# Top-k attention: the steering rounds moved from ScalarE's tile counts to TensorE differences with one Sign per head

## Chip, cores and metric

One core of a Trainium2 chip runs the whole program. The metric is the device time of one execution in microseconds (us), lower is better. The kernel before takes 3272.49 us (median of 3 runs, 3266.62 to 3277.44).

## What is computed

A block over 32 batches of 256 tokens and 256 features: a layernorm, a cross attention with 16 heads of 16 features in which each query keeps only its 64 highest scores, a gated residual, a second layernorm, an 8-bit float matrix product with bias, and a second gated residual.

```python
scores = jnp.einsum('bhqd,bhkd->bhqk', Q, K) / sqrt(d)          # 256 x 256 per batch and head
topk_scores, topk_idx = jax.lax.top_k(scores, 64)
probs = jax.nn.softmax(topk_scores, axis=-1)
attn = einsum('bhqk,bhqkd->bhqd', probs, gather(V, topk_idx))
x = x + tanh(g_xattn) * (attn @ Wo.T + bo)
x = x + tanh(g_ffn) * ffn_fp8(layernorm(x))
```

## The kernel before, in words

**Groups and tiles.** Half of a batch's heads (8 of 16) make a *group*; there are 64 groups, numbered `i`. A head has 256 queries by 256 keys of scores, which are two *tiles* of 128 queries by 256 keys, so a group has 16 tiles (`GT`). `score_sb` holds four groups of tiles (`RING`) in the SBUF, queries on the partitions.

**Finding the 64th score.** For every query row a threshold `X` is looked for in four steering rounds (`GUIDES`), `r` = 0 to 3. A round counts how many scores of each row lie above `X` and moves `X` toward the count 60.5 (`AIM`) by a Newton or a chord step. After the four rounds the scores above `X` are counted once more and the eight next lower ones are picked with MAX8 (`following`); count and place give the 64th score exactly, `thr`. Rows whose 64th and 65th scores tie are *unsure* and are settled by a slow path (`settle`, `select_tile`).

**Who does what.** In `guide_counts` (L880) ScalarE counts 15 of the 16 tiles of a round: a `Sign` of X minus the tile, with `accum_out` as the count. VectorE counts the 16th (L1068). VectorE then moves the thresholds in `update_thresholds` (L1083 to L1121), a chain of up to eight dependent steps on 16 or 32 columns, between whose steps two `copy_scores` are placed. `final_tiles` (VectorE) makes for four tiles a round a compare with count (L1146), one pass over 1024 columns that turns the scores above X into -3e38 (L1151), and four MAX8 (L1157). `final_thresholds` closes a group.

ScalarE also makes the masks, `unfit` = Relu(thr - score), (`masks_of`, L891) and the exponentials `pT_sb` (`exps`, L900), and evacuates the projections, the mixed values and the MLP. TensorE computes the scores (`scores`, L698), the transposed scores with the masks added times `dropb` (`exponents`, L712 and L716), the product with the values (`mix`, L731, in float32, recorded as two matmuls each), and the projections. VectorE copies the scores from the PSUM with their row maximum (`copy_scores`, L1047). SP moves the operands through DRAM; GpSimd does layernorms and splits operands into bf16 parts.

**Order.** All orders are written out by hand, one stream for each engine, with semaphores between them. While VectorE finishes group `i`, the rounds steer group `i + 1`, the scores of group `i + 2` are copied, and group `i - 1` is masked, exponentiated and mixed. So a batch is eight rounds long (`g` = 0, 1; `r` = 0 to 3), and the program has 256 of them. Each round of ScalarE is:

```python
                        if guided:
                            guide_counts(2 * b + g + 1, (2 * p + g + 1) % RING, r)
                        for n in (2 * r, 2 * r + 1):
                            if mixes:
                                masks_of(2 * mb + mg, 2 * mp + mg, n)
                                mixing(mb, mp, mu, mg, n, has(-1))
```

and TensorE does in it, for two heads, scores, exponents and mix, plus one of the projections in some rounds. In the PSUM, `ps_s` (scores) and `ps_e` (exponents) have two banks each, and `ps_o`, `ps_a`, `ps_b`, `ps_x` one each.

## Time and profile before

| | before |
|---|---|
| median of 3 runs | 3272.49 us |
| the profiled execution's own time | 3268.81 us |
| its span | 3266.9 us |
| busy: VectorE, ScalarE | 2691.6 us (82%), 2730.3 us (84%) |
| busy: TensorE matmuls, weight loads | 1780.4 us (54%), 950.5 us (29%) |
| busy: GpSimd | 966.1 us (30%) |
| mean granted TensorE clock | 0.717 of 2.4 GHz |

Busy time is the union of an engine's instructions; it does not say which engine the others wait for. Instructions of one engine overlap by a part of their latency, so a group's mean duration is longer than the step from one start to the next, and a sum over a stream has to be made with steps between starts. TensorE's clock is granted at one of two levels, 0.50 (1.2 GHz) or 1.00 (2.4 GHz); a number between them for a stretch is a mean over time.

### The profile page before, as it was taken

The numbers are of one execution on the slowest core, as the hardware profiler recorded it, in microseconds if no ns is written. First come the engines' busy times: TensorE is split into PE (matmuls) and PEld (weight loads), VectorE is DVE, ScalarE is ACT, GpSimd is POOL, SyncE is SP. The second block draws the span as 40 slices with busy tenths as digits, with TensorE's granted clock in tenths as the row PEclk, the third lists the DMA queues.
The fourth block names the chain that finished last, engine by engine and source line by source line (L and its number), as shares of the span: only waits on it lengthen the run. The fifth ranks groups of instructions, "written<-read, shape, count | busy, mean of one in ns | idle before, by whom it ended". The sixth has DMA issues, their size and how long they took to land.

```text
span 3266.9 us, 51511 instructions
## 1 busy us (share of the span) xinstructions
PE 1780.4 (54%) x7952; PEld 950.5 (29%) x7952; DVE 2691.6 (82%) x11883; ACT 2730.3 (84%) x9638; POOL 966.1 (30%) x1174
## 2 busy tenths in 40 slices
PE   3245555555465555455556556564556556454555
PEld 2122233332233233232323333332233223232222
DVE  1678888888888888888888888888888888888884
ACT  1888888998788898797889998988798788997983
POOL 5122223233222233232233223333223233232112
PEclk8567677777677777776667777767676767777777
DMA  4223332223333223331233333223333133331211
GB/s 70 38 43 60 49 47 52 52 49 63 52 52 54 45 49 63 52 55 34 48 64 56 60 48 56 48 48 64 53 49 55 33 62 61 55 54 33 40 24 46
DMA packets 451902, 166.43 MB, mean 51 GB/s; under 512 B 245616, under 2 KB 451440, under 8 KB 451520
## 3 DMA queue, kind: packets, MB, share of 16 engines
q1 hardware_dynamic: 451136, 162.38, 28.4%
q14 instruction: 310, 2.54, 0.3%
q8 instruction: 72, 1.18, 0.2%
q0 software_dynamic: 384, 0.33, 0.1%
HBM read 102.57 MB, written 59.24 MB: 50 GB/s over the span
## 4 chain that ended last, share of the span: by engine, by line
DVE 36%; ACT 30%; issue 17%; PE 14%; DVEq 2%; POOL 1%; ACTq 0%; DMA 0%; SPq 0%; POOLq 0%; another core or an unknown queue 0%
ACT act_junk L880 22%; DVE masked L1151 5%; DVE score_sb L1047 4%; PE ps_o L731 4%; DVE following L1157 4%; DVE masked L1146 3%; ACT unfit L891 3%; ACT pT_sb L900 2%; PE ps_a L684 2%; DVE X L1083 2%; PE ps_b L675 2%; PE ps_e L712 1%; PE ps_a L686 1%; DVE chord L1115 1%; PE ps_e L716 1%
## 5 line engine op out<-in xcount | busy, mean ns | idle before, releaser
L880 ACT ACTIVATE act_junk<-score_sb,X 128x256 int8<-128x256 f32 x3840 | 1892.1, 503 | 211.3 <-DVE X L1121 183.2
L712 PE MATMUL ps_e<-qs,ks 99*128 99x256 bf16 x1024 | 348.2, 350 | 1321.7 <-ACT pT_sb L900 1321.7
L731 PE MATMUL ps_o<-pT_sb,v_aug 128*32 128x256 f32 x2048 | 766.4, 514 | 0.5 <-ACT pT_sb L900 0.5
L880 ACT ACTIVATION_READ_ACCUMULATOR act_junk<-score_sb,X 128x1 f32 x3840 | 755.0, 197 | 0.0
L891 ACT ACTIVATE unfit<-score_sb,thr 128x256 bf16<-128x256 f32 x1024 | 463.1, 504 | 218.0 <-DVEq L1241 214.6
L1047 DVE TENSOR_SCALAR_CACHE_REDUCE score_sb<-ps_s 128x256 f32<-128x256 f32 x1024 | 418.8, 415 | 142.1 <-PE ps_s L698 140.0
L712 PEld LDWEIGHTS ps_e<-qs,ks 99*128 99x128 bf16 x1024 | 121.9, 119 | 1403.6 <-ACT unfit L891 1199.5
L1146 DVE TENSOR_SCALAR_CACHE_REDUCE masked<-score_sb,X 128x256 f32<-128x256 f32 x1024 | 426.3, 472 | 19.1 <-DVE x_res L1294 8.4
L1157 DVE MAX8 following<-masked 128x8 f32<-128x256 f32 x1024 | 357.7, 409 | 1.7 <-issue 0.7
L540 POOL CAST split<-proj 128x512 bf16<-128x512 f32 x64 | 48.0, 750 | 1042.8 <-ACT proj L866 1027.2
L716 PE MATMUL ps_e<-dropb,unfit 128*128 128x128 bf16 x2048 | 355.9, 273 | 0.0
L1151 DVE SCALAR_TENSOR_TENSOR masked<-masked,score_sb 128x1024 f32<-128x1024 f32 x256 | 336.8, 1316 | 0.4
L900 ACT ACTIVATE pT_sb<-ps_e 128x512 f32<-128x512 f32 x512 | 301.7, 590 | 11.9 <-PE ps_o L731 11.8
L731 PEld LDWEIGHTS ps_o<-pT_sb,v_aug 128*32 128x32 f32 x2048 | 231.9, 136 | 266.4 <-issue 191.0
L716 PEld LDWEIGHTS ps_e<-dropb,unfit 128*128 128x128 bf16 x2048 | 253.3, 124 | 52.4
L698 PE MATMUL ps_s<-ks,qs 96*128 96x256 bf16 x1024 | 228.2, 311 | 67.7 <-DVE score_sb L1047 35.1
L1083 DVE TENSOR_TENSOR X<-aim,count 128x16 f32<-128x16 f32 x256 | 82.3, 322 | 200.8 <-ACT act_junk L880 167.3
L510 POOL TENSOR_SCALAR var<-mv 128x2 f32<-128x2 f32 x64 | 14.6, 228 | 579.4 <-DVE mv L994 576.5
L1068 DVE SCALAR_TENSOR_TENSOR dve_junk<-score_sb,X,minus_twos 128x256 bf16<-128x256 f32 x256 | 158.2, 618 | 0.1
L698 PEld LDWEIGHTS ps_s<-ks,qs 96*128 96x128 bf16 x1024 | 74.8, 102 | 269.8 <-issue 206.2
L602 POOL TENSOR_TENSOR rest<-y_sb,magic_sb 128x512 f32<-128x512 f32 x32 | 43.9, 1371 | 362.4 <-DVE magic_sb L1020 362.4
L559 POOL COPY qs<-rows 96x4096 bf16<-96x4096 bf16 x32 | 127.2, 3974 | 22.7 <-DMA rows<-q_scr 11.6
(158 smaller groups left out, 3332.8 us busy)
## 6 DMA issues: line engine op xcount, KB each, us to landing
rows<-q_scr SPq DMA_DIRECT2D x192, 128.0 KB, 5.1
rows<-k_scr SPq DMA_DIRECT2D x192, 128.0 KB, 5.0
o_scr<-o_sb SPq DMA_DIRECT2D x128, 128.0 KB, 2.7
q_scr<-split SPq DMA_DIRECT2D x32, 384.0 KB, 2.7
k_scr<-split SPq DMA_DIRECT2D x32, 384.0 KB, 2.7
x_in<-in_x SPq DMA_DIRECT2D x32, 256.0 KB, 3.1
ctx_sb<-in_ctx SPq DMA_DIRECT2D x32, 256.0 KB, 2.7
v_scr<-proj SPq DMA_DIRECT2D x32, 256.0 KB, 5.8
```

What stands on the lines that cost most here:

```text
L698: ins = nc.tensor.matmul(ps_s[:, n % 2, jh * TOK:(jh + 1) * TOK], qs[u][0:SPLITS, h, 8 * jh:8 * jh + 8, :].rearrange("d j t -> d (j t)"), ...
L712: nc.tensor.matmul(ps_e[:, n % 2, kc * TOK:(kc + 1) * TOK], ks[u][:, h, 8 * kc:8 * kc + 8, :].rearrange("d j t -> d (j t)"), qs[u][:, h, : ...
L716: ins = nc.tensor.matmul(ps_e[:, n % 2, kc * TOK + jh * P:kc * TOK + jh * P + P], unfit[:, n % MASKS, jh, kc * P:kc * P + P], dropb[:], st ...
L731: ins = nc.tensor.matmul(ps_o[32 * c:32 * c + 32, half * TOK:(half + 1) * TOK], v_aug[p][:, 2 * h + kc, :], pT_sb[:, n % 2, kc * TOK:(kc + ...
L880: ins = nc.scalar.activation(act_junk[:, t, :], score_sb[:, slot, t, :], ACT.Sign, scale=-1.0, bias=X[slot % 2][:, 0, t:t + 1], accum_out= ...
L891: ins = nc.scalar.activation(unfit[:, n % MASKS, jh, :], score_sb[:, slot, t, :], ACT.Relu, scale=-1.0, bias=thr[:, slot, t:t + 1])
L900: nc.scalar.activation(pT_sb[:, n % 2, :], ps_e[:, n % 2, :], ACT.Exp).then_inc(s_PT, 1)
L1047: ins = nc.vector.tensor_scalar(score_sb[:, slot, t, :], ps_s[:, n % 2, jh * TOK:(jh + 1) * TOK], 0.0, None, ALU.add, ALU.max, accum_out=m ...
L1068: ins = nc.vector.scalar_tensor_tensor(dve_junk[:, t - ACT_TILES, :], score_sb[:, slot, t, :], X[slot % 2][:, 0, t:t + 1], minus_twos[:].t ...
L1146: nc.vector.tensor_scalar(masked[:, k, :], score_sb[:, slot, t, :], X[slot % 2][:, 0, t:t + 1], None, ALU.is_gt, ALU.add, accum_out=final_ ...
L1151: nc.vector.scalar_tensor_tensor(masked[:], masked[:], -BIG, scores, ALU.mult, ALU.add).then_inc(s_fin, 1)
L1157: nc.vector.max(following[:, t, 1:], masked[:, k, :]).then_inc(s_fin, 1)
```

## The change

**Steering rounds.** TensorE writes for each head the transposed scores S^T (keys on the partitions, 256 queries; two matmuls) into one of three PSUM banks `ps_t`, and adds minus the thresholds of the queries to them by two more matmuls over 16 rows (`less_thresholds`). For that the thresholds are transposed by TensorE (`transpose_thresholds`) and negated into bf16 by ScalarE (`negate_thresholds`). ScalarE takes one `Sign` of 512 columns for a head, from the PSUM, without a count (`signs`), and TensorE sums the signs over the keys with a ones vector, four matmuls of one column for a head (`tally`). VectorE reads the counts from the PSUM.

**Final count and finals.** ScalarE counts four tiles a round with `Sign` and `accum_out` (`final_counts`). VectorE's pass becomes one instruction a tile, (score <= X) * score, in place of the compare and the 1024-column pass; `final_thresholds` gets two more small steps.

**Masks.** `masks_of` moves to VectorE: bf16 compares score < thr.

**Order and PSUM.** Exponents share the three banks with the differences; mix is lagged by 2 heads, both exponents and mix. `ps_b` and `ps_x` are gone, so that all projections and the MLP go through `ps_a`, one after the other, and stand behind the count part of a round in TensorE's stream. Their evacuations stand behind ScalarE's count part. On VectorE all four `copy_scores` of a round, and its four masks, stand ahead of `update_thresholds`, whose steps no longer have copies between them. `store_values` is split from `move_values` on SP and issued earlier; `move_out` goes ahead of `move_values`.

The core of the diff:

```diff
-MASK_LAG, MIX_LAG = 2, 4
+MIX_LAG = 2
+BANKS = 3
+SIGNS = 3
+JUNK = 4
...
+            def transpose_thresholds(i, slot, r):
+                pe.wait_ge(s_thr, GUIDES * i + r + 1)
+                pe.wait_ge(s_crd, GUIDES * i + r)
+                nc.tensor.transpose(ps_xt, X[slot][:, 0, :], ident[:]).then_inc(s_xt, 1)
+            def scores_by_key(u, g, n, bank):
+                h = head_of(g, n)
+                for kc in range(2):
+                    nc.tensor.matmul(ps_t[:, bank, kc * TOK:(kc + 1) * TOK],
+                                     ks[u][0:SPLITS, h, 8 * kc:8 * kc + 8, :].rearrange("d j t -> d (j t)"),
+                                     qs[u][0:SPLITS, h, :, :].rearrange("d j t -> d (j t)"), start=(kc == 0), stop=False,
+                                     skip_group_check=True)
+            def less_thresholds(i, r, n, bank):
+                if n == 0:
+                    pe.wait_ge(s_mx, GUIDES * i + r + 1)
+                both_chunks = minus_x[:].rearrange("t (o q) -> t o q", o=1).to_broadcast([GT, 2, P])
+                for jh in range(2):
+                    ins = nc.tensor.matmul(ps_t[:, bank, :].rearrange("p (c j q) -> p c j q", c=2, j=2)[:, :, jh, :],
+                                           identb[0:GT, 2 * n + jh:2 * n + jh + 1].to_broadcast([GT, P]), both_chunks,
+                                           start=False, stop=(jh == 1), skip_group_check=True)
+                ins.then_inc(s_R, 1)
+            def tally(i, par, r, n, buf):
+                pe.wait_ge(s_G, GUIDES * GH * i + GH * r + n + 1)
+                for jh in range(2):
+                    for kc in range(2):
+                        ins = nc.tensor.matmul(ps_cnt[par][:, 2 * n + jh:2 * n + jh + 1],
+                                               sign[:, buf, kc * TOK + jh * P:kc * TOK + jh * P + P], ones_b[:],
+                                               start=(kc == 0), stop=(kc == 1))
+                if n == GH - 1:
+                    ins.then_inc(s_cnt, 1)
...
+            def count_round(b, p, u, g, r, phase, first, second, last, middle):
...
+                scores_by_key(u, g, 0, bank[0])
+                scores_by_key(u, g, 1, bank[1])
+                less_thresholds(i, r, 0, bank[0])
+                less_thresholds(i, r, 1, bank[1])
+                if last:
+                    exponent_taken(*last)
+                for n in (2, 3):
+                    scores_by_key(u, g, n, bank[n])
+                    less_thresholds(i, r, n, bank[n])
+                    tally(i, slot % 2, r, n - 2, buf[n - 2])
+                if first:
+                    exponents(*first, bank[4], False)
+                if middle:
+                    middle()
+                for n in (4, 5):
+                    tally(i, slot % 2, r, n - 2, buf[n - 2])
+                    scores_by_key(u, g, n, bank[n + 1])
+                    less_thresholds(i, r, n, bank[n + 1])
+                if first:
+                    exponent_taken(*first)
+                for n in (6, 7):
+                    scores_by_key(u, g, n, bank[n + 1])
+                    less_thresholds(i, r, n, bank[n + 1])
+                    tally(i, slot % 2, r, n - 2, buf[n - 2])
+                if second:
+                    exponents(*second, bank[9], False)
+                for n in (6, 7):
+                    tally(i, slot % 2, r, n, buf[n])
...
-            def guide_counts(i, slot, r):
-                for t in range(ACT_TILES):
-                    ins = nc.scalar.activation(act_junk[:, t, :], score_sb[:, slot, t, :], ACT.Sign, scale=-1.0,
-                                               bias=X[slot % 2][:, 0, t:t + 1], accum_out=count[slot % 2][:, t:t + 1])
-                ins.then_inc(s_cnt, 1)
...
+            def negate_thresholds(i, r):
+                act.wait_ge(s_xt, GUIDES * i + r + 1)
+                nc.scalar.activation(minus_x[:], ps_xt, ACT.Copy, scale=-1.0).then_inc(s_mx, 1)
+            def signs(i, r, n, buf, bank):
+                act.wait_ge(s_R, GUIDES * GH * i + GH * r + n + 1)
+                nc.scalar.activation(sign[:, buf, :], ps_t[:, bank, :], ACT.Sign).then_inc(s_G, 1)
+            def final_counts(i, slot, t):
+                if t == 0:
+                    act.wait_ge(s_fin, FINAL * i + 1)
+                if t % JUNK == 0:
+                    act.wait_ge(s_fc, 4 * i + t // 4)
+                ins = nc.scalar.activation(act_junk[:, t % JUNK, :], score_sb[:, slot, t, :], ACT.Sign, scale=-1.0,
+                                           bias=X[slot][:, 0, t:t + 1], accum_out=final_count[:, t:t + 1])
+                if t % 4 == 3:
+                    ins.then_inc(s_fc, 1)
...
-                    nc.vector.tensor_scalar(masked[:, k, :], score_sb[:, slot, t, :], X[slot % 2][:, 0, t:t + 1], None,
-                                            ALU.is_gt, ALU.add, accum_out=final_count[:, t:t + 1]).then_inc(s_fin, 1)
+                    nc.vector.scalar_tensor_tensor(masked[:, k, :], score_sb[:, slot, t, :], X[slot][:, 0, t:t + 1],
+                                                   score_sb[:, slot, t, :], ALU.is_le, ALU.mult).then_inc(s_fin, 1)
                 yield
                 dve.wait_ge(s_fin, base + QUARTER)
-                scores = score_sb[:, slot, q * QUARTER:(q + 1) * QUARTER, :]
-                nc.vector.scalar_tensor_tensor(masked[:], masked[:], -BIG, scores,
-                                               ALU.mult, ALU.add).then_inc(s_fin, 1)
...
+            def masks_of(i, slot, n):
+                H = GH * i + n
+                dve.wait_ge(s_T, at(H - MASKS + 1))
+                carry(dve)
+                for jh in range(2):
+                    t = 2 * n + jh
+                    ins = nc.vector.tensor_scalar(unfit[:, n % MASKS, jh, :], score_sb[:, slot, t, :], thr[:, slot, t:t + 1], None,
+                                                  ALU.is_lt)
+                ins.then_inc(s_P, 1)
```

**TensorE, one round in the middle of the program, before.** Two heads of scores (`ps_s`), exponents (`ps_e`) and mix (`ps_o`), with an output projection (`ps_x`) between them:

```order
L698 MATMUL ps_s<-ks,qs 128x256 [waits scores_copied]
L698 MATMUL ps_s<-ks,qs 128x256
L712 MATMUL ps_e<-qs,ks 128x256 [waits probs_ready,masks_ready]
L716 MATMUL ps_e<-dropb,unfit 128x128 x2
L712 MATMUL ps_e<-qs,ks 128x256
L716 MATMUL ps_e<-dropb,unfit 128x128 x2
L731 MATMUL ps_o<-pT_sb,v_aug 32x256 [waits probs_ready]
L731 MATMUL ps_o<-pT_sb,v_aug 32x256
```

These rows stand twice in a round and, with one projection, are all of it.

**The same engine after the change, the start of a round.** `ps_c` holds transposed thresholds and counts, `ps_t` the three banks:

```order
L737 MATMUL ps_c<-ident,X 16x128 [waits counts_read,thresholds_moved]
L743 MATMUL ps_t<-qs,ks 128x256 x4
L754 MATMUL ps_t<-minus_x,identb 128x2x128 [waits thresholds_negated]
L754 MATMUL ps_t<-minus_x,identb 128x2x128 x3
...
L743 MATMUL ps_t<-qs,ks 128x256 x2
L754 MATMUL ps_t<-minus_x,identb 128x2x128 x2
L764 MATMUL ps_c<-ones_b,sign 128x1 [waits signs_ready]
L764 MATMUL ps_c<-ones_b,sign 128x1 x3
L780 MATMUL ps_t<-qs,ks 128x256 [waits masks_ready]
L784 MATMUL ps_t<-dropb,unfit 128x128 x2
```

The per-head work of steering now stands on TensorE ahead of the scores and mix of the round, and each head's counts wait for ScalarE's signs.

**ScalarE, one round, before and after.** Before:

```order
L880 ACTIVATE act_junk,count<-score_sb,X 128x256 x15
L888 REGISTER_ALU
L891 ACTIVATE unfit<-score_sb,thr 128x256 x2
L898 REGISTER_ALU
L900 ACTIVATE pT_sb<-ps_e 128x512
L891 ACTIVATE unfit<-score_sb,thr 128x256 x2
L898 REGISTER_ALU
L900 ACTIVATE pT_sb<-ps_e 128x512
```

After, from a round's start on:

```order
L1020 ACTIVATE minus_x<-ps_c 16x128
...
L1025 ACTIVATE sign<-ps_t 128x512
...
L1025 ACTIVATE sign<-ps_t 128x512
L1033 ACTIVATE act_junk,final_count<-score_sb,X 128x256
...
L1025 ACTIVATE sign<-ps_t 128x512
...
L1025 ACTIVATE sign<-ps_t 128x512
...
L1043 ACTIVATE pT_sb<-ps_t 128x512
L1033 ACTIVATE act_junk,final_count<-score_sb,X 128x256
```

Fifteen counts in a row without a wait inside became eight signs, each of which waits for TensorE, with final counts and exponentials between them.

## Rows read from the trace of the kernel before

**Rows 1.** The page: span and busy time of each engine.

```profile
span 3266.9 us, 51511 instructions
PE 1780.4 (54%) x7952; PEld 950.5 (29%) x7952; DVE 2691.6 (82%) x11883; ACT 2730.3 (84%) x9638; POOL 966.1 (30%) x1174
```

**Rows 2.** One instruction a batch (L1247): count, first and last start.

```profile
L1247 DVE STREAM_TRANSPOSE topT<-top x32: 202/205/211, 129.3 to 3143.6; 128x32 f32<-128x32 f32 x32
```

**Rows 3.** ScalarE groups: busy and mean ns | idle before, releaser.

```profile
L880 ACT ACTIVATE act_junk<-score_sb,X 128x256 int8<-128x256 f32 x3840 | 1892.1, 503 | 211.3 <-DVE X L1121 183.2
L891 ACT ACTIVATE unfit<-score_sb,thr 128x256 bf16<-128x256 f32 x1024 | 463.1, 504 | 218.0 <-DVEq L1241 214.6
```

**Rows 4.** ScalarE in order of time: start, duration.

```profile
1752.14 0.91 ACT L891 ACTIVATE unfit<-score_sb,thr 128x256 bf16<-128x256 f32 x2
1752.94 0.59 ACT L900 ACTIVATE pT_sb<-ps_e 128x512 f32<-128x512 f32 x1
1755.09 0.51 ACT L880 ACTIVATE act_junk<-score_sb,X 128x256 int8<-128x256 f32 x1 [1.56 <-DVE X L1121]
```

**Rows 5.** VectorE in order of time, an update of the thresholds with one copy inside shown.

```profile
1762.83 0.17 DVE L1083 TENSOR_TENSOR X<-aim,count 128x16 f32<-128x16 f32 x1 [1.26 <-ACT act_junk L880]
...
1763.95 0.41 DVE L1047 TENSOR_SCALAR_CACHE_REDUCE score_sb<-ps_s 128x256 f32<-128x256 f32 x1
...
1765.63 0.18 DVE L1121 COPY_PREDICATED X<-both,chord 128x16 f32<-128x16 int32 x1
```

**Rows 6.** VectorE groups that the change removes, and the nearest to what it adds.

```profile
L1146 DVE TENSOR_SCALAR_CACHE_REDUCE masked<-score_sb,X 128x256 f32<-128x256 f32 x1024 | 426.3, 472 | 19.1 <-DVE x_res L1294 8.4
L1151 DVE SCALAR_TENSOR_TENSOR masked<-masked,score_sb 128x1024 f32<-128x1024 f32 x256 | 336.8, 1316 | 0.4
L1068 DVE SCALAR_TENSOR_TENSOR dve_junk<-score_sb,X,minus_twos 128x256 bf16<-128x256 f32 x256 | 158.2, 618 | 0.1
L1015 DVE TENSOR_SCALAR masked<-y_sb 128x512 int32<-128x512 int32 x33 | 13.9, 420 | 0.0
```

**Rows 7.** TensorE groups: its longest wait, and the masks' weight loads.

```profile
L712 PE MATMUL ps_e<-qs,ks 99*128 99x256 bf16 x1024 | 348.2, 350 | 1321.7 <-ACT pT_sb L900 1321.7
L716 PEld LDWEIGHTS ps_e<-dropb,unfit 128*128 128x128 bf16 x2048 | 253.3, 124 | 52.4
```

**Rows 8.** TensorE in order of time, at 1.2 GHz.

```profile
1787.27 0.37 PE L712 MATMUL ps_e<-qs,ks 99*128 99x256 bf16 x1 [6.14 <-ACT pT_sb L900]
...
1788.21 1.92 PE L731 MATMUL ps_o<-pT_sb,v_aug 128*32 128x256 f32 x4
1790.05 1.52 PE L684 MATMUL ps_a<-wT,cT 128*128 128x256 f32 x4
```

**Rows 9.** The same, some us later, at 2.4 GHz.

```profile
1793.81 0.39 PE L698 MATMUL ps_s<-ks,qs 96*128 96x256 bf16 x2
1794.04 0.27 PE L712 MATMUL ps_e<-qs,ks 99*128 99x256 bf16 x1
1794.15 0.28 PE L716 MATMUL ps_e<-dropb,unfit 128*128 128x128 bf16 x2
1794.27 0.27 PE L712 MATMUL ps_e<-qs,ks 99*128 99x256 bf16 x1
...
1794.59 1.05 PE L731 MATMUL ps_o<-pT_sb,v_aug 128*32 128x256 f32 x4
1795.57 0.39 PE L698 MATMUL ps_s<-ks,qs 96*128 96x256 bf16 x2
```

**Rows 10.** Stretches: us, busy (x) of PE, PEld, DVE, ACT, POOL, PEclk.

```profile
1725.80:1728.70 2.90, 0.00 (x0) 0.00 (x1) 2.19 (x13) 2.90 (x11) 0.00 (x0) 1.00 0.00 0
1730.00:1732.50 2.50, 2.50 (x7) 1.42 (x6) 2.50 (x12) 2.50 (x10) 2.19 (x3) 0.50 0.00 0
1796.00:1797.20 1.20, 0.01 (x1) 0.05 (x2) 1.20 (x5) 1.20 (x4) 0.00 (x0) 1.00 0.52 167
1797.20:1800.00 2.80, 2.80 (x22) 1.99 (x23) 2.73 (x12) 1.60 (x4) 1.27 (x1) 1.00 0.26 90
```

More of the change, by code:

```diff
@@ L120, in build @@
         AB = sb("AB", [P, 2, GT])
-        count = [sb(f"count{k}", [P, GT]) for k in range(2)]
-        aim = sb("aim", [P, GT])
+        sign = sb("sign", [P, SIGNS, 2 * TOK], BF16)
+        minus_x = sb("minus_x", [GT, P], BF16)
         newton = sb("newton", [P, GT])
@@ L1381, in _ @@
             invert(NB - 2)
+            for n in range(4, GH):
+                masks_of(2 * NB - 1, RING - 1, n)
             finish(NB - 3, 1, FINAL * 2 * NB)
```

505 lines of the change are left out of this document (284 added, 221 removed).

## Prediction

> **What bounds the kernel now.** The page's busy times come first [rows 1]: VectorE 82% and ScalarE 84%, TensorE 54%. Neither leader is full, so I look for a cycle. One instruction a batch on VectorE gives the beat [rows 2]: 32 of them between 129.3 and 3143.6 us, so 3014.3 / 31 = 97.2 us a batch and **12.15 us a round** (eight a batch). The 252.6 us outside those 31 batches are start and end. ScalarE is busy 2730.3 / 256 = 10.7 us a round: 15 counts at 1892.1 / 3840 = 0.49 us, 7.4 [rows 3]; two pairs of masks at 0.80 from start to next (1752.14 to 1752.94), though a pair is 0.91 long, so about 0.1 overlaps [rows 4], 1.6; two exponentials, 0.59 long, so about 0.48 in step, 1.0; and 0.7 of evacuations and the like. Some 1.7 us a round it is idle, for moved thresholds and for settled rows (211.3 + 218.0 us over 256 rounds) [rows 3]. So ScalarE's length plus the turn through VectorE's update, 2.98 us from 1762.83 to 1765.81 with two copies inside of 0.41, about 0.34 in step [rows 5], sets the beat. TensorE waits 1321.7 us for exponentials [rows 7] and is no bound.
>
> **The change, engine by engine, per round.** *ScalarE:* 15 counts and four masks go (7.4 + 1.6). Eight signs of 512 columns come; the exponential has their shape and source, 0.48 each, 3.8; four final counts at 0.49, 2.0; one negation of 16 x 128, 0.3. ScalarE falls from 10.7 to 7.8 us, some 2000 us in all.
>
> *VectorE:* the compares, the 1024-column pass and the count go: 426.3 + 336.8 + 158.2 = 921 us [rows 6]. The new pass has 1024 instructions of two sources; a quarter of the old pass is 0.33, the count of one tile 0.62: 340 to 630 us, I take 400. The masks have 1024 instructions; a one-source pass over 512 columns takes 0.42 [rows 6], so 0.2 to 0.47 each, 205 to 480 us, I take 260, near the lower end since the columns are half. VectorE falls to about 2430 us (2320 to 2880). Its update chain loses the two copies: 2.3 us in rounds 1 and 2 of a group, about 1.2 in round 0 (no chord), and in round 3 only the first step stands before the next group's thresholds.
>
> *TensorE* gets the work. At 2.4 GHz a 256-column matmul steps in 0.11 (1794.04 to 1794.15), one head's exponents take 0.55 (1794.04 to 1794.59), one head's mix 0.98 (1794.59 to 1795.57), a head's scores 0.23 [rows 9]. A round then has: keyed scores 16 x 0.11 = 1.8; minus thresholds 16 x 0.11 = 1.8; 32 tallies; exponents 1.1; mix 2.0; scores 0.5; projections, MLP and transposes about 1.2; transposed thresholds 0.3. The tally has no row of its own: a full weight load with one column behind it. Two weight loads with 128 columns each step in 0.12 [rows 9] (1794.15 to 1794.27), so 0.06 is the nearest row; the weight load's own row is 0.124 with its latency [rows 7]. I take 0.06, 1.9 a round, and keep 0.03 (if one column is cheaper than 128) and 0.124 as ends: 1.0 to 4.0. Sum: **10.6 us of TensorE a round**, where 54% of 12.15 was 6.6. The Trainium skill, TensorE: Matmul & The Clock Gate, "LDWEIGHTS (loading the stationary operand)", prices a load at its columns over 1.2 GHz, 107 ns for 128, whatever the rows; by that the tallies would be 3.4 us and the round 1.5 longer. By that rule, too, the pairs at 1794.15 could not step as they do, so the trace disagrees at the higher clock.
>
> *The turn.* From negated thresholds to the last sign ScalarE needs about 0.3 + 3.8 + 0.5 (one exponential) + 1.5 (three final counts) = 6.2 us, and TensorE 5.8 in the same stretch (six keyed heads 1.3, eight minus thresholds 1.8, exponents 1.1, seven tallies of four 1.6), in a ring of three banks. Then tally 0.4, VectorE 2.3, transpose and negation 0.8: 9.7 us. But behind the last tally TensorE has mix, scores and often a projection: 2.0 + 0.5 + 1.2 = 3.7 us, more than VectorE's 2.3. So **TensorE becomes the bound**: 10.6 plus 0.6 in which it waits for the negation and the first and last signs, 11.2 us at 2.4 GHz all the time. Nothing hides its clock any more.
>
> *The clock.* Before, its mean of 0.717 says 57% of the time at the lower level. The trace shows full clock kept over a gap of 1.2 us (1796.0 to 1797.2) and held while the engine works on, and also half clock while fully busy (1730.0 to 1732.5) after it had been idle from 1725.8 to 1728.7 [rows 10]. The new round has no idle stretch of 3 us, so I expect it mostly full, but with a fall now and then in the stretch of short waits on signs. At 1.2 GHz exponents take 0.94 and mix 1.84 [rows 8] against 0.55 and 0.98, so a us at half clock loses about half a us. I take a mean of 0.94: 10.6 / 0.94 + 0.4 = 11.7 us a round.
>
> *Queues.* SP's earlier store of the values and the moves in another order cost nothing: their cover is a whole batch, 97 us. The single bank `ps_a` puts each projection behind the last one's evacuation, but one round, 11 us, lies between. `prepare_rounding` (eight dependent passes, the one over 512 columns 0.42 [rows 6]; I estimate 4 us) stands behind the update of round 0 and ahead of the final passes of round 1: VectorE then needs some 10 us where 7 to 9 are there, 0.2 us a round on the mean; it lies within the 0.4.
>
> Sum: 31 batches x 8 x 11.7 = 2902 us, plus 252.6 of start and end, where the masks that VectorE now makes (16 at 0.25) and the first rounds, which nothing overlaps, change less than 10 us: a span of 3154. The profiled execution took 1.9 us more than its span (3268.81) and was 0.1% under the median, so the forecast is **3160 us**.
>
> **The rivals.**
> (A) *The clock keeps falling.* TensorE now waits for ScalarE in each of eight heads, and half of its new columns runs over 16 rows only. The mechanism: the clock falls in the count stretch, the tail (mix, projections) runs at 1.2 GHz until it rises again, and nobody covers that time, since TensorE is the bound. A round is 10.6 / c + 0.4; the point from which the change is slower is c = 0.90 (12.15 us). At c = 0.83 it is 13.2 us, 248 x 13.2 + 253 = 3520 us; at the old mean of 0.72, 15.1 us, 4000. For it: the clock of before falls in nearly each round. Against it: there it has gaps of 3 to 6 us. The Trainium skill, same page, "A second HAM failure mode: psum-queue depth-cycling", says that a kernel which cycles PSUM banks can oscillate between the clock's levels through short idles between groups of matmuls; three banks in a ring are such a case. Chance 0.38, most of it between 3290 and 3560.
> (B) *Full clock and cheap tallies.* At 0.03 a tally TensorE's round is 9.7 + 0.6, near the turn's 9.7: 10.4 us, 248 x 10.4 + 253 = 2830 us. Chance 0.17.
> (C) *VectorE binds.* With its upper ends, 2880 us busy and the update that waits for counts in each round, 12.15 us a round: 3266 us, no change. Against it: its middle is 2430. Chance 0.05.
> (D) *The work is only moved.* TensorE at its upper tally price (4.0 us a round) at full clock: 12.7 + 0.6 = 13.3, 3550 us. Chance 0.05.
>
> **How the numbers follow.** The forecast, 3160 with its own range of 2950 to 3250 (c from 0.90 to 1.0), has 0.35; A 0.38, B 0.17, C 0.05, D 0.05. Faster by over 0.3% (what a measurement of this kernel can tell) takes the forecast and B, 0.52; the same is C with the edges of the others, 0.04; slower is A, D and some of C, 0.44. The range has to leave out 0.2: I cut the lower half of B at 2840 and A and D from 3580 on.
>
> **What would show it.** TensorE at 85 to 95% busy, with its 1321.7 us of waiting for exponentials gone; ScalarE near 2000 us, VectorE near 2430; the sign at 0.48 from start to start; the pass at about 0.33 to 0.4; tallies at 0.06; a beat of 11.7 us a round. The mean clock decides: above 0.90 the forecast, below it A. If TensorE is under 80% busy and ScalarE waits for moved thresholds as before, the turn binds and my bound is wrong. If the clock is full and the time still above 3262, it is tallies (D) or waits in the ring of banks that I set too low.

## The result: 2.88 times as long

| | before | after |
|---|---|---|
| median | 3270.86 us (3266.62 to 3277.44, 4 runs) | 9411.05 us (9397.62 to 9414.13, 4 runs) |
| ratio, 95% interval | | 2.876 [2.870, 2.882] |
| span of the profiled execution | 3266.9 us | 9412.3 us |
| mean granted TensorE clock | 0.717 | 0.566 |

The forecast was 3160 us with a range up to 3580. It was wrong in its sign and far off in its size. The page of after, its head, answers to [rows 1]:

```profile
span 9412.3 us, 104413 instructions
PE 3607.8 (38%) x24592; PEld 1793.1 (19%) x24592; DVE 7174.0 (76%) x26768; ACT 2136.9 (23%) x5286; POOL 916.1 (10%) x1172
DVE  3777777777777777777777777777777777777776
PEclk6555555555555555555555555555555555555555
```

ScalarE is at 2137 us where 2000 were forecast, but VectorE is busy for 7174 us in 26768 instructions, where it had 11883 before. The groups of the page (busy, mean ns | idle before, releaser) say with what; L1025 stands for the counts of [rows 3], L1368 for their masks, L1299 for the pass of [rows 6]:

```profile
L737 PE MATMUL ps_c<-ident,X 128*16 128x128 f32 x256 | 88.3, 345 | 5467.8 <-DVE X L1256 5458.0
L1352 DVE MAX8 max<-masked 128x8 f32<-128x256 f32 x4504 | 1926.7, 428 | 156.2
L1354 DVE MATCH_REPLACE8 masked<-max,masked 128x256 f32<-128x256 f32 x4504 | 1839.4, 408 | 0.0
L1025 ACT ACTIVATE sign<-ps_t 128x512 bf16<-128x512 f32 x2048 | 1164.8, 603 | 442.0 <-PE ps_t L754 440.2
L1347 DVE TENSOR_SCALAR thr<-thr x563 | 86.6, 154 | 741.2 <-issue 741.2
L1299 DVE SCALAR_TENSOR_TENSOR masked<-score_sb,X 128x256 f32<-128x256 f32 x1024 | 426.4, 477 | 17.8 <-DVE x_res L1467 9.1
L1368 DVE TENSOR_SCALAR unfit<-score_sb,thr 128x256 bf16<-128x256 f32 x1024 | 360.3, 413 | 40.8 <-DVE score_sb L1356 36.9
```

L1347 to L1356 are `select_tile`, the slow path. It ran for 563 tiles of 1024. TensorE's transpose of the thresholds (L737) waits 5458 us for VectorE, most of the 6140 us that were added. One such tile in VectorE's timeline (start, duration):

```profile
4003.10 0.15 DVE L1347 TENSOR_SCALAR thr<-thr  x1 [1.22 <-issue]
4003.25 0.38 DVE L1349 COPY masked<-score_sb 128x256 f32 x1
4003.66 0.43 DVE L1352 MAX8 max<-masked 128x8 f32<-128x256 f32 x1
...
4011.53 0.38 DVE L1356 TENSOR_SCALAR score_sb<-masked 128x256 f32 x1
4013.14 0.15 DVE L1347 TENSOR_SCALAR thr<-thr  x1 [1.23 <-issue]
```

From start to start a tile takes 4013.14 - 4003.10 = 10.04 us, with eight MAX8 and eight replacements in series and 1.2 us of loop. The kernel before did it for 7 tiles:

```profile
L1187 DVE TENSOR_SCALAR thr<-thr x7 | 1.1, 154 | 12.1 <-issue 12.1
```

In 20 us of this path, read off as one stretch, no other engine runs and the clock is at its lower level. In the 2.9 us of idle TensorE in [rows 10] it was still at the higher one; here TensorE is idle for all of the 20 (us, busy of PE, PEld, DVE, ACT, POOL, PEclk):

```profile
3990.00:4010.00 20.00, 0.00 (x0) 0.00 (x0) 16.40 (x54) 0.00 (x0) 0.00 (x0) 0.50 0.00 0
```

So 556 more tiles by 10.04 us are 5582 us of the 6140 that the change costs (an estimate, if all tiles cost as much as this one). Two questions follow: why so many tiles are unsure, and what the other 560 us are.

### The profile page after: what moved, and what is told of

It is laid out like the page before. It is cut to its first block and busy times, and to the rows that moved or that the text cites. A ratio compares the mean times of both kernels' runs of the same rounds, so it can differ in the third digit from the quotient of the medians.

```text
span 9412.3 us, 104413 instructions
## 1 busy us (share of the span) xinstructions
PE 3607.8 (38%) x24592; PEld 1793.1 (19%) x24592; DVE 7174.0 (76%) x26768; ACT 2136.9 (23%) x5286; POOL 916.1 (10%) x1172
## 5 line engine op out<-in xcount | busy, mean ns | idle before, releaser
L737 PE MATMUL ps_c<-ident,X 128*16 128x128 f32 x256 | 88.3, 345 | 5467.8 <-DVE X L1256 5458.0
L1352 DVE MAX8 max<-masked 128x8 f32<-128x256 f32 x4504 | 1926.7, 428 | 156.2
L1354 DVE MATCH_REPLACE8 masked<-max,masked 128x256 f32<-128x256 f32 x4504 | 1839.4, 408 | 0.0
L1020 ACT ACTIVATE minus_x<-ps_c 16x128 bf16<-16x128 f32 x256 | 68.2, 266 | 6032.6 <-PE ps_c L737 6032.6
L1025 ACT ACTIVATE sign<-ps_t 128x512 bf16<-128x512 f32 x2048 | 1164.8, 603 | 442.0 <-PE ps_t L754 440.2
L737 PEld LDWEIGHTS ps_c<-ident,X 128*16 128x16 f32 x256 | 26.8, 105 | 5502.4 <-DVE X L1256 5479.1
L754 PE MATMUL ps_t<-minus_x,identb 16*128 16x256 bf16 x4096 | 972.3, 338 | 0.0
L743 PE MATMUL ps_t<-qs,ks 96*128 96x256 bf16 x4096 | 967.8, 340 | 0.6 <-issue 0.5
L1347 DVE TENSOR_SCALAR thr<-thr x563 | 86.6, 154 | 741.2 <-issue 741.2
L1354 DVE MATCH_VALUE_LOAD masked<-max,masked 128x8 f32 x4504 | 414.8, 92 | 155.3
L1033 ACT ACTIVATE act_junk<-score_sb,X 128x256 int8<-128x256 f32 x1024 | 527.9, 516 | 7.5 <-DVE following L1296 7.3
L764 PE MATMUL ps_c<-ones_b,sign 128*128 128x1 bf16 x8192 | 504.1, 169 | 8.8 <-ACT sign L1025 8.2
L764 PEld LDWEIGHTS ps_c<-ones_b,sign 128*128 128x128 bf16 x8192 | 382.3, 106 | 432.8 <-ACT sign L1025 285.0
L1299 DVE SCALAR_TENSOR_TENSOR masked<-score_sb,X 128x256 f32<-128x256 f32 x1024 | 426.4, 477 | 17.8 <-DVE x_res L1467 9.1
L1368 DVE TENSOR_SCALAR unfit<-score_sb,thr 128x256 bf16<-128x256 f32 x1024 | 360.3, 413 | 40.8 <-DVE score_sb L1356 36.9
```

Source lines behind the costliest of these rows:

```text
L743: nc.tensor.matmul(ps_t[:, bank, kc * TOK:(kc + 1) * TOK], ks[u][0:SPLITS, h, 8 * kc:8 * kc + 8, :].rearrange("d j t -> d (j t)"), qs[u][0 ...
L754: ins = nc.tensor.matmul(ps_t[:, bank, :].rearrange("p (c j q) -> p c j q", c=2, j=2)[:, :, jh, :], identb[0:GT, 2 * n + jh:2 * n + jh + 1 ...
L764: ins = nc.tensor.matmul(ps_cnt[par][:, 2 * n + jh:2 * n + jh + 1], sign[:, buf, kc * TOK + jh * P:kc * TOK + jh * P + P], ones_b[:], star ...
L1025: nc.scalar.activation(sign[:, buf, :], ps_t[:, bank, :], ACT.Sign).then_inc(s_G, 1)
L1033: ins = nc.scalar.activation(act_junk[:, t % JUNK, :], score_sb[:, slot, t, :], ACT.Sign, scale=-1.0, bias=X[slot][:, 0, t:t + 1], accum_o ...
L1299: nc.vector.scalar_tensor_tensor(masked[:, k, :], score_sb[:, slot, t, :], X[slot][:, 0, t:t + 1], score_sb[:, slot, t, :], ALU.is_le, ALU ...
```

## Experiments

A row is unsure not only when its 64th and 65th scores tie: `final_thresholds` gives up too where the final count is outside the window of eight ranks. My theory for the tiles was a difference of arithmetic. The steering rounds of after compare with minus X rounded to bf16 (`minus_x`), the final count and the pass with X in float32; a row that steering left at the window's edge then counts one more or less and falls out. One such row sends its tile of 128 rows down the slow path. The rival S on record was the new final pass, which writes zeros for the scores above X where the old one wrote -3e38. Two more are the Sign on the PSUM and the order of the additions there.

### e1: X rounded once, at the end of steering

```diff
+                    nc.vector.tensor_copy(rounded[:], x[:, 0, :]).then_inc(s_upd, 1)
+                    dve.wait_ge(s_upd, 8)
+                    nc.vector.tensor_copy(x[:, 0, :], rounded[:]).then_inc(s_upd, 1)
+                    dve.wait_ge(s_upd, 9)
```

> The changed kernel; after the fourth steering round VectorE rounds the thresholds X to bf16 once and writes them back (two steps of 16 columns per group), so that the final count and the final pass use the very values that the steering compared with. Theory R (rounding): rows leave the window of eight ranks because the steering compares with -X in bf16 and the finals with X in float32; then the slow path runs for about 5 tiles and not 563 (a count made from the inputs in ordinary arithmetic gives 562 tiles for the changed kernel, 7 for the one before, 5 for this one). At 10.03 us a tile (4003.10 to 4013.14 in the trace of the changed kernel) the time is 9411 - 558 x 10.03 = 3815 us. Rival S (the sign of the scores): the new final pass writes zeros for the scores above X where the old one wrote -3e38, so rows whose next scores are not positive fail; then rounding changes nothing and the time stays at 9400 us.

Measured: 3805.57 us, ratio to before 1.162 [1.159, 1.164]. The slow path is gone, down to the 7 tiles of before:

```profile
L1352 DVE TENSOR_SCALAR thr<-thr x7: 153/154/154, 391.5 to 3463.8; - x7
```

Two copies of 16 columns in the last round of a group take 5605 us away. Final count and steering now use the same number. The new final pass, the Sign on the PSUM and the order of the additions are still in e1, so none of them is the cause.

### e2: a narrower window for steering

```diff
-                    nc.vector.tensor_scalar(far_f[:], square[:], (WINDOW - 1) ** 2 + 0.5, None, ALU.is_gt)
+                    nc.vector.tensor_scalar(far_f[:], square[:], (WINDOW - 3) ** 2 + 0.5, None, ALU.is_gt)
```

(and the same in `far`.)

> The changed kernel; steering goes on unless the count is within 2.5 ranks of the aim and not 3.5 (two constants), so that a row seldom stands at the edge of the window when its threshold is rounded. Theory R: 69 slow tiles by the count from the inputs, so 3815 + 64 x 10.03 = 4460 us, on one line with the changed kernel and the one that rounds once. Rival S: nothing changes, 9400 us. If the slow tiles are 69 and the time is well above 4460, the slow path costs more than its own 10 us, through the engines that it makes wait.

Measured: 4478.64 us, 1.368 [1.364, 1.373], with 70 slow tiles. A row that steering leaves a rank inside the edge mostly survives the rounding, as the theory says. 63 more tiles than in e1 by 10.04 us are 632 us, and 3806 + 632 = 4438; the 41 us left are within 1%.

### e3: the kernel before, with rounded thresholds for the counts of steering alone

```diff
-                                               bias=X[slot % 2][:, 0, t:t + 1], accum_out=count[slot % 2][:, t:t + 1])
+                                               bias=XR[slot % 2][:, t:t + 1], accum_out=count[slot % 2][:, t:t + 1])
```

`XR` is X copied to bf16 and back after every update.

> The kernel before, order and engines untouched; only the thresholds that the steering counts compare with are rounded to bf16 (two more steps of 16 columns behind each update), while the updates and the finals keep X in float32. Theory R: about 562 slow tiles, 3270 + 555 x 10.03 + about 100 us for the steps = 8940 us. If the new order or the new final pass is the cause (rival S), it stays near 3370 us with 7 slow tiles.

Measured: 9131.86 us, 2.790 [2.784, 2.795]. Of the change this kernel has only the rounding in the steering counts, and it has the same number of slow tiles as after (its group of the same instruction):

```profile
L1203 DVE TENSOR_SCALAR thr<-thr x563 | 86.6, 154 | 730.9 <-issue 730.9
```

With e1 this settles the cause of the slow path: steering compares with a rounded X and the final count with an unrounded one. The PSUM, the Sign, the final pass and the order are not needed for it. 556 tiles by 10.04 us give 3271 + 5582 = 8853 us; the 279 us above that were not taken apart (each update has two more dependent copies here).

### e4 and e6: the same products over more rows

With the slow path gone, e1 is still 16% slower than before. TensorE is now 93% busy at a granted 0.652, and that makes it the likely bound:

```profile
PE 3568.1 (93%) x24592; PEld 1794.6 (47%) x24592; DVE 2543.4 (67%) x11371; ACT 2131.0 (56%) x5286; POOL 919.7 (24%) x1172
PEclk8556666666666666666666666666676667666666
```

The forecast's rival A had named one possible reason: half of the new columns runs over 16 rows only. e4 is e1 with these matmuls over 128 rows, of which 112 are zeros. Columns, instructions and results stay.

```diff
-        minus_x = sb("minus_x", [GT, P], BF16)
+        minus_x = sb("minus_x", [P, P], BF16)
...
-                both_chunks = minus_x[:].rearrange("t (o q) -> t o q", o=1).to_broadcast([GT, 2, P])
+                both_chunks = minus_x[:].rearrange("t (o q) -> t o q", o=1).to_broadcast([P, 2, P])
...
-                                           identb[0:GT, 2 * n + jh:2 * n + jh + 1].to_broadcast([GT, P]), both_chunks,
+                                           identb[:, 2 * n + jh:2 * n + jh + 1].to_broadcast([P, P]), both_chunks,
```

> The kernel that rounds once, with the matmuls that subtract the thresholds run over all 128 rows (16 of them hold thresholds and the others zeros) and not over 16: same columns, same results. It tests what is left over once the slow path is gone, some 550 us against the kernel before. Theory C (clock): TensorE binds and its clock stays low because half of its new columns use 16 rows; then the mean clock rises clearly and the time falls by 100 us or more against the run that rounds once. Rival O (order): the remainder is waits in the chain of a round, and the time is the same within 0.5%, whatever the clock does.

Measured: 3322.24 us, 1.015 [1.012, 1.017], at a clock of 0.883. Work on zeros saves 483 us, so theory C holds: TensorE was the bound of e1, and the waits on the signs and the ring of three banks, which e4 has too, are not what held its clock at 0.652. e6 has 64 rows in the same place.

> The kernel that rounds once, the thresholds subtracted over 64 rows (48 of them zeros), the old place of the sum. Between 16 rows (3806 us, clock 0.652) and 128 rows (3322 us, 0.883). Theory C with a graded effect of the rows: in between, near 3500 us and 0.78. If it were any fixed property of the 16-row form (its broadcast weights or its load), 64 rows would already give the 3322 us.

Measured: 3552.53 us, 1.085 [1.081, 1.090], clock 0.789. The traces show that two things are at work. First, TensorE in order of time in stretches at a granted 1.00, in e1 (16 rows), in e6 (64) and in e4 (128). The step is the time from the start of one row to the start of the next:

```profile
1705.65 0.38 PE L744 MATMUL ps_t<-qs,ks 96*128 96x256 bf16 x2
1705.96 0.39 PE L755 MATMUL ps_t<-minus_x,identb 16*128 16x256 bf16 x2
1706.28 0.25 PE L765 MATMUL ps_c<-ones_b,sign 128*128 128x1 bf16 x4
1706.40 0.27 PE L781 MATMUL ps_t<-qs,ks 99*128 99x256 bf16 x1
```

```profile
1500.09 0.38 PE L745 MATMUL ps_t<-qs,ks 96*128 96x256 bf16 x2
1500.40 0.39 PE L756 MATMUL ps_t<-minus_x,identb 64*128 64x256 bf16 x2
1500.72 0.25 PE L766 MATMUL ps_c<-ones_b,sign 128*128 128x1 bf16 x4
```

```profile
1609.53 0.38 PE L745 MATMUL ps_t<-qs,ks 96*128 96x256 bf16 x2
1609.74 0.38 PE L756 MATMUL ps_t<-minus_x,identb 128*128 128x256 bf16 x2
1609.96 0.38 PE L745 MATMUL ps_t<-qs,ks 96*128 96x256 bf16 x2
```

A pair steps in 0.31 to 0.32 us in e1 and e6, in 0.21 to 0.22 in e4: each passage from 96 rows to 16 or 64, and each back to 96 or 128, costs 0.1 us. It costs as much at a granted 0.50, where a pair steps in 0.53 to 0.54 us in e1 and in 0.42 to 0.43 in e4:

```profile
1624.26 0.61 PE L744 MATMUL ps_t<-qs,ks 96*128 96x256 bf16 x2
1624.80 0.60 PE L755 MATMUL ps_t<-minus_x,identb 16*128 16x256 bf16 x2
1625.33 0.26 PE L765 MATMUL ps_c<-ones_b,sign 128*128 128x1 bf16 x4
```

```profile
1630.45 0.63 PE L745 MATMUL ps_t<-qs,ks 96*128 96x256 bf16 x2
1630.87 0.63 PE L756 MATMUL ps_t<-minus_x,identb 128*128 128x256 bf16 x2
1631.30 0.29 PE L766 MATMUL ps_c<-ones_b,sign 128*128 128x1 bf16 x4
```

A round has seven such stretches, 14 passages, 1.4 us, some 360 us of TensorE's time in all. The weight load of L755 shows the same as idle time, 497.7 us put down to issue, and none in e4. The Trainium skill, TensorEngine Tiling (Array Packing), "Key Properties", says that a change of the tiling mode drains TensorE; a drain at each passage is what these steps look like, but no run separates it from another cost at the same place. Second, e6 has the passages of e1 and is still 253 us faster, by its clock (0.789 against 0.652).

### e13 and e14: 96 and 32 rows

> The kernel that rounds X once (3806 us with 16 rows), with the matmuls of minus the thresholds over 96 rows (80 of them zeros). The traces of 16, 64 and 128 rows show two things apart: at the granted clock of 1.00 a pair of these matmuls, and the pair of keyed scores ahead of it, steps in 0.32 us with 16 and with 64 rows and in 0.22 with 128 (a step of 0.1 us at each change of the row count), and the clock's mean is 0.652, 0.789 and 0.883. Theory S (what costs 0.1 us is a change of the size class of the array between 64 and less and more than 64 rows, and the keyed scores with 96 rows are of the same class as 128): pairs of 0.22 us, and with them most of the step from 64 to 128 rows: 3330 to 3400 us, clock 0.85 to 0.89. Theory R (each change of the row count costs, 128 against 96 too, and 128 rows are cheap only by being full): pairs of 0.32 us, and a time between those of 64 and 128 rows, 3430 to 3500 us.

> The same with 32 rows (16 of them zeros). Theory P (the mean clock follows the number of rows that the new matmuls run over): from 16 rows at 0.652 and 64 at 0.789, 0.137 over 48 rows, 32 rows give 0.70 and a third of the 253 us, 3720 us. Theory Q (the clock steps with size classes, and 16 and 32 rows are one): 0.65 and 3806 us as with 16 rows. Pairs step at 0.32 us at the clock of 1.00 in both.

| rows of the new matmuls | 16 | 32 | 64 | 96 | 128 |
|---|---|---|---|---|---|
| kernel | e1 | e14 | e6 | e13 | e4 |
| median, us | 3805.57 | 3764.72 | 3552.53 | 3389.01 | 3322.24 |
| mean granted clock | 0.652 | 0.675 | 0.789 | 0.835 | 0.883 |
| step of a pair at 1.00, us | 0.32 | 0.32 | 0.32 | 0.22 | 0.22 |

The same rows of TensorE at a granted 1.00 in e13 (96 rows) and e14 (32):

```profile
1009.88 0.38 PE L745 MATMUL ps_t<-qs,ks 96*128 96x256 bf16 x2
1010.09 0.38 PE L756 MATMUL ps_t<-minus_x,identb 96*128 96x256 bf16 x2
1010.31 0.38 PE L745 MATMUL ps_t<-qs,ks 96*128 96x256 bf16 x2
```

```profile
1003.93 0.38 PE L745 MATMUL ps_t<-qs,ks 96*128 96x256 bf16 x2
1004.24 0.39 PE L756 MATMUL ps_t<-minus_x,identb 32*128 32x256 bf16 x2
1004.56 0.25 PE L766 MATMUL ps_c<-ones_b,sign 128*128 128x1 bf16 x4
```

The ratios to before are 1.039 [1.035, 1.042] for e13 and 1.152 [1.150, 1.154] for e14. Theory S holds for the steps: with 96 rows they are 0.22 us (so the passage to 128 rows is free, and the line lies between 64 and 96). For the clock, 32 rows came out between P (3720) and Q (3806): it rises with the rows at every step, but not in proportion. From 96 to 128 rows the steps don't change and the time falls by 67 us, so this part is the clock's alone. The step from 64 to 96 rows, 164 us, is less than the 360 us that the passages add up to, so not all of their time was on the path. How the 164 us divide between passages and clock is not known, since without the passages the clock has another history too. Why the clock follows the rows stays open: the runs show that it does, and no more.

### e5, e7 and e8: a wait that only moves

e4 is still 1.5% slower than before. In its timeline the first round of nearly each group, one round in four, has a gap of some 2.5 us, 148 us in 58 waits, where TensorE's sum of the unsure rows (L881) waits for VectorE in the middle of the signs:

```profile
1606.01 0.28 PE L786 MATMUL ps_t<-dropb,unfit 128*128 128x128 bf16 x2
1608.74 0.20 PE L881 MATMUL ps_s<-unsure_b,ones_c 128*1 128x16 f32 x2 [2.45 <-DVE score_sb L1213]
```

e5 moves this sum behind the last difference of the round, and its two readers on VectorE with it; e7 does the same in e1.

```diff
-                if middle:
-                    middle()
                 for n in (4, 5):
...
+                if middle:
+                    middle()
                 if second:
```

> The kernel that rounds once with full rows; the sum of the unsure rows moves in TensorE's stream from the middle of round 0 of a group to behind the last difference, and VectorE reads it behind the second pair of copies and not ahead of the first MAX8. In the run with full rows TensorE stood 148.1 us in 58 waits at this matmul for the first score copy of the round, 2.5 us a group, with four keyed heads, five signs and the tallies queued behind it. Theory W (that wait lies on the path since TensorE binds): 110 to 148 us less, 3322 - 130 = 3190 us, 2.5% under the kernel before. Rival D (VectorE binds in round 0, the wait only shows it): VectorE still comes late to the counts of round 0 and less than 40 us are won.

> The same new place of the sum, but with the thresholds subtracted over 16 rows as in the changed kernel. With theory C (the clock falls for want of rows) the clock stays near 0.65 and the time near 3806 less at most 130, about 3700 us. If the stall at the sum had been what made the clock fall, the clock would rise above 0.75 and the time fall below 3550 us.

Measured: e5 3334.98 us, 1.020 [1.018, 1.021], and e7 3827.72 us, 1.170 [1.164, 1.175]. A miss: the wait for the copy is gone and no time was won, since TensorE waits elsewhere instead. Its tallies wait 277.9 us for signs (187.5 in e4) and its transposes of the thresholds 303.9 us for VectorE (239.6 in e4), 155 us more together for the 148 that went. ScalarE's negation waits 674.6 us for the transpose (598.1 in e4). That is rival D: VectorE is late in that round, and TensorE's gap only showed it. e7 had less to win, since this wait was 35 us in e1 and not 148. Its clock stays at 0.653, so a stall at the sum is not what lowers the clock. e8 takes work out of VectorE's late rounds: it is e5 with the range check of the token rounding (a pass over 512 columns) two rounds later.

> The kernel with the sum later; the range check of the MLP's input (five of the eight passes behind round 0's update, 1616.59 to 1619.4 in the run with full rows, 2.9 us) moves to behind round 2's update. It is VectorE's work ahead of the final passes of round 1, where VectorE comes last. If VectorE's lateness costs in round 1 only, up to 1.5 us a batch, 30 to 50 us less than the run with the sum later. If TensorE binds there too, nothing.

Measured: 3315.75 us, 1.014 [1.011, 1.016], 19 us under e5 where 30 to 50 were expected.

### e9, e10 and e11: which engine is it now?

e9 is e4 with the later range check alone:

```diff
-                            prepare_rounding(b - 3, FINAL * i + 2 * QUARTER + 1)
+                            prepare_rounding(b - 3)
+                        if has(-3) and (g, r) == (0, 2):
+                            check_range(b - 3, FINAL * i + 6 * QUARTER + 1)
```

> The kernel with 128 rows and X rounded once (3322 us), with one edit: the range check of the token rounding (a pass over 512 columns and its sums) stands two rounds later on VectorE, the middle sum stays where it was. Theory C (VectorE's update comes late in the first rounds of a batch, and each us of lateness is a us of the round): the edit with the moved sum gave 19 us, so the same here, 3303 us. Theory D (what that edit gained came from the clock alone, 0.887 to 0.900): also some 19 us, but with a higher granted clock. Either way it stays above the kernel before (3272).

e10 makes VectorE lighter (masks over 2 of 256 columns), e11 makes ScalarE heavier (one more Sign over 16 columns ahead of each final count), both on e9.

> The same kernel, with the masks of all but the first four heads computed over 2 of 256 columns (it leaves out the rest of each mask, so the attention weights are not the reference's); all instructions and waits stay. It takes from VectorE some 1024 x (0.375 - 0.1) = 280 us, 1.1 us a round. Theory C (VectorE's late update is what keeps a round at 12.2 us at a clock of 0.88): the round falls by most of it, to 11.2 to 11.6 us, 3050 to 3150 us. Theory E (the chain of signs and tallies between TensorE and ScalarE and the clock bind; VectorE is late in one round of eight only): a gain of 0 to 60 us, 3240 to 3300 us.

> The same kernel as the first of this call, with one more Sign over 16 columns ahead of each of ScalarE's four final counts a round (its result is not used): some 0.2 us each, 0.9 us a round, 230 us in all on ScalarE, which is 62% busy. Theory E (ScalarE stands in the chain between a difference and its tally): 120 to 230 us more, 3420 to 3530 us. Theory C (VectorE or TensorE's own length binds, ScalarE has room): under 60 us more, 3300 to 3360 us.

Measured: e9 3307.05 us, 1.010 [1.008, 1.012]; e10 3224.32 us, 0.985 [0.981, 0.988]; e11 3356.46 us, 1.026 [1.024, 1.028]. e9 is 15 us under e4 at the same clock (0.882 to 0.888 in its runs, 0.883 to 0.890 in e4's), so it is theory C and not D. Busy times and the masks' group in e9, then the same in e10, then the busy times of e11:

```profile
PE 2609.5 (79%) x24592; PEld 1792.9 (54%) x24592; DVE 2611.3 (79%) x11371; ACT 2068.1 (63%) x5286; POOL 922.6 (28%) x1173
```

```profile
L1374 DVE TENSOR_SCALAR unfit<-score_sb,thr 128x256 bf16<-128x256 f32 x1024 | 387.6, 439 | 62.4 <-issue 47.2 <-PE ps_t L786 11.2 <-DVE score_sb L1362 3.9
```

```profile
PE 2562.4 (79%) x24592; PEld 1763.6 (55%) x24592; DVE 2477.0 (77%) x11371; ACT 2062.5 (64%) x5286; POOL 919.6 (28%) x1173
```

```profile
L1375 DVE TENSOR_SCALAR unfit<-score_sb,thr 128x2 bf16<-128x2 f32 (+1 forms) x1024 | 256.6, 319 | 64.5 <-issue 34.7 <-PE ps_t L786 25.9 <-DVE score_sb L1362 3.9
```

```profile
PE 2607.0 (78%) x24592; PEld 1776.2 (53%) x24592; DVE 2622.9 (78%) x11371; ACT 2246.6 (67%) x6310; POOL 922.3 (28%) x1173
```

I had expected the narrow masks to take 280 us from VectorE; they took 134. Four masks in a row, in e9 and in e10, show why:

```profile
1529.41 1.13 DVE L1374 TENSOR_SCALAR unfit<-score_sb,thr 128x256 bf16<-128x256 f32 x4
1533.75 0.62 DVE L1375 TENSOR_SCALAR unfit<-score_sb,thr 128x2 bf16<-128x2 f32 x4
```

With medians of 0.346 and 0.224 us for one mask, the steps between starts are 0.26 and 0.13 us, and 1024 x 0.13 is the 134. The means of the groups, 0.439 and 0.319, are higher because some masks last up to 2.9 us: in e9 118 of the 1024 are more than 15% over the median, and each of them overlaps a GpSimd instruction; of the 767 that overlap none, the longest took 0.354 us. No run took GpSimd's work away, so this is where the long ones stand and not yet a shown cause.

So 83 us of time came with 134 us taken from VectorE, 0.6 a us. On ScalarE 178 us more (2068.1 to 2246.6 busy) cost 49, 0.3 a us. For e11 that is theory C. For e10 the time lies in neither range (3050 to 3150 for C, 3240 to 3300 for E); C fits if its saving is scaled to what was really removed. The clock of e10 rose too, from 0.888 to 0.905, and how much of the 83 us is the clock's was not separated. VectorE's stream is on the path for the greater part, ScalarE's for the smaller.

### e12 and e15: masks back to ScalarE, faster than before

These prices point at a version. e12 gives one of each head's two masks back to ScalarE as Relu(thr - score), at the end of its round, e15 both.

```diff
+            def second_mask(i, slot, n):
+                H = GH * i + n
+                t = 2 * n + 1
+                act.wait_ge(s_sel, i + 1)
+                act.wait_ge(s_T, at(H - MASKS + 1))
+                nc.scalar.activation(unfit[:, n % MASKS, 1, :], score_sb[:, slot, t, :], ACT.Relu, scale=-1.0,
+                                     bias=thr[:, slot, t:t + 1]).then_inc(s_PA, 1)
```

> The kernel with 128 rows, X rounded once and the range check two rounds later (3307 us), with one of the two masks of each head moved back to ScalarE, at the end of its round, as Relu(threshold - score): 512 of VectorE's 1024 mask instructions (387.6 us busy) go, some 194 us, and 512 instructions of 0.42 us, some 215 us, come to ScalarE. From the two runs before it: 131 us taken from VectorE gave 83 us (0.63 us a us), and 181 us added to ScalarE cost 49 us (0.27 a us). Theory C (VectorE's stream is now for the most part on the path, ScalarE's for a quarter): -122 + 58 = -64 us, 3243 us, faster than the kernel before (3272) by 0.9%. Theory E (the gain of the narrow masks came from a better clock, not from VectorE): no gain or a loss, 3307 to 3365 us.

> The kernel with 128 rows, one rounding of X, the later range check and half of the masks on ScalarE (3231 us), with the other half moved to ScalarE too. VectorE gives up some 130 us more, ScalarE takes some 190 (2257 to 2450 busy, 76% of the span). By the prices of the runs before (0.6 us for each us taken from VectorE, 0.27 for each added to ScalarE): -78 + 51 = -27 us, 3204 us. Rival: ScalarE, which holds the chain of signs, is now the later one and each of its us counts: 3231 to 3330 us.

Measured: e12 3230.53 us, 0.987 [0.985, 0.989]; e15 3182.29 us, 0.974 [0.972, 0.975]. e12 is 77 us under e9 where 64 were expected, and e15 gave 48 us more where 27 were expected. The prices served to rank the versions, not as constants: e12 took 129 us from VectorE and not 194, and with that its sum comes to less than 30 us. The page of e15:

```profile
span 3175.9 us, 85604 instructions
PE 2533.8 (80%) x24592; PEld 1741.1 (55%) x24592; DVE 2292.1 (72%) x10347; ACT 2441.8 (77%) x6310; POOL 914.3 (29%) x1173
```

The three busy engines are nearly even now, VectorE at 72% (from 79%), ScalarE at 77% (from 63%), TensorE at 80% at a granted 0.92. So the idea of the change is worth 2.6% here, with X rounded once, full rows, the later range check, and its masks left where they were. The later range check gave 15 us in e9 and was not tried in the kernel before; the 2.6% can hold that much of something else.

## Why the prediction was wrong

**The settled rows.** This is the step that failed. The prediction speaks of settled rows once, as a wait of ScalarE before the change, and the changed kernel's slow path has no term and no rival: it was put at nothing more than before, without a reason. The change compares with a bf16 number in steering where it had been a float32 one, and so 563 tiles take the slow path and not 7. 5605 of the 6140 us are this (e1), and e3 has it without the rest of the change.

**The clock.** This is the second term that failed. The sum took a mean of 0.94; without the slow path it is 0.652 (e1). Rival A had the fall of the clock on a bound TensorE, and named three things for it: waits for ScalarE, the matmuls over 16 rows, and three banks in a ring. e4 keeps the first and the third and runs at 0.883, so the rows are the reason. A expected 3290 to 3560 us for the most part; e1 is at 3806. Its formula gives 10.6 / 0.652 + 0.4 = 16.7 us a round, where e1's batches are (3677.6 - 170.2) / 31 = 113.1 us, 14.1 a round:

```profile
L1425 DVE STREAM_TRANSPOSE topT<-top x32: 211/211/213, 170.2 to 3677.6; 128x32 f32<-128x32 f32 x32
```

**TensorE's length.** A pair over 256 columns was taken at 0.22 us; it steps in 0.32 next to the 16-row pair, 1.4 us a round that no term had. With full rows it is 0.22 as forecast. The tally, taken at 0.06 us with ends of 0.03 and 0.124, is at the lower end: four step in 0.12 (1706.28 to 1706.40), 0.03 each, which is rival B's price and takes 1 us from the sum. TensorE is busy 2609.5 / 256 = 10.2 us a round in e9 at a clock of 0.888; by the prediction's own rule (length divided by clock) that is an estimate of 9.1 us at full clock, where the sum had 10.6. So the sum was some 1.5 us too long, and with 9.1 the formula above gives 14.4 for e1, near the 14.1, though without the passages.

**ScalarE and VectorE.** ScalarE is at 2068 us in e9 and was forecast at 2000. The sign, forecast at 0.48 from start to start, is 0.48 there (0.60 in its own row). VectorE was forecast at 2430 and is at 2611. Its new pass was forecast at 400 us and the masks at 260. From start to start they are what was forecast (medians of 0.40 and 0.26 us, 405 and 269 us), but their groups are busy for 527.6 and 387.6 us, since some of the passes, like the masks above, last up to 1.5 us:

```profile
L1305 DVE SCALAR_TENSOR_TENSOR masked<-score_sb,X x1024: 386/479/1517, 148.4 to 3224.9; 128x256 f32<-128x256 f32 x171
```

All 125 long passes overlap a GpSimd instruction. With the two faults mended, e9's batch is

```profile
L1426 DVE STREAM_TRANSPOSE topT<-top x32: 211/212/214, 155.0 to 3169.4; 128x32 f32<-128x32 f32 x32
```

(3169.4 - 155.0) / 31 = 97.2 us, 12.15 a round, exactly the beat before [rows 2]. It is also the number of rival C (VectorE binds, 5%), but by luck: C asked for 2880 us of VectorE and for each us of it to count, and the runs show 2611 us and a price of 0.6.

**Start and end.** They were forecast to change by less than 10 us. In e9 they are 3306.0 - 3014.4 = 292 us, before 252.6: 39 us more, of which 26 stand ahead of the first of these instructions (155.0 against 129.3) and 13 behind the last. They cover the 33 us that e9 loses to the kernel before (3307.05 against 3273.79 measured beside it). Why they grew was not looked at further.

**Small slips.** The prediction's formula gives about 3270 us at c = 0.90, where its own range ends at 3250, and the turn's 6.2 us add up to 6.1. Neither matters beside the two terms above.

**What would show it.** Of the signs that the prediction listed, two were right to name: TensorE under 80% busy (38%) said that its bound was wrong, and the clock decided between the forecast and A, for the part that is not the slow path. ScalarE's negation waits 6032.6 us for the transposed thresholds in after, the sign that the turn binds; it does so because of the settled tiles within it.

## What to carry to other kernels

Where a change touches the precision of a number that decides a branch, count how often the branch is taken before and after: one threshold in two formats turned 7 slow tiles into 563, and no busy time of the old profile shows it. A matmul over few rows beside ones over many can be the dearer one; zeros up to the full height gave 483 us here. And a wait seen on one engine is worth its length only if nothing behind it is late as well: price an engine by adding or removing a known amount of its work, and take the price as a guide to the next version and not as a constant.

## What the runs showed of the hardware

- The mean granted clock of TensorE rose with the rows of half of the new 256-column matmuls, 0.652, 0.675, 0.789, 0.835 and 0.883 for 16, 32, 64, 96 and 128 rows (e1, e14, e6, e13, e4), with the same matmuls and waits in the program. TensorE was 93% busy in e1, with the lowest clock, and 78% in e4.
- Going between matmuls over 96 or 128 rows and over 16, 32 or 64 rows costs 0.1 us each way, in e1 at either level of the clock; between 96 and 128 (e4, e13) it costs nothing that shows.
- A full weight load with one column behind it steps in 0.03 us (four in 0.12, e1).
- A compare on VectorE steps in 0.26 us over 256 columns (e9) and in 0.13 over 2 (e10), with medians of 0.346 and 0.224 us in their own rows. The ones that lasted up to 2.9 us all overlap a GpSimd instruction.
